# Third stage of a two-layer decoder on one core: the product of memory scores and decay goes from VectorE to GpSimd

## What is computed

```
lfm   = csum[:, :, :, None] - csum[:, :, None, :]        # csum of log sigmoid(forget gate)
log_D = where(lower triangle, lfm, -inf) + ig[:, :, None, :]
D     = exp(log_D - max(log_D, axis=-1))
C     = (q @ k.T / 4 + k_hop) * D                         # the product that is moved
h     = C / (max(|sum(C)|, exp(-max log_D)) + 1e-6) @ v
h     = per-head layer norm of h
x     = layernorm(x + h)
```

## Time and profile before

| | us |
|---|---|
| runs, median of 3 | 4131.79 (4114.9 to 4133.13) |
| the profiled execution | 4115.69 |
| its span, first to last instruction | 4113.5 |
| third stage, within the span | about 894 to 1890 |

### The profile page before, as it was taken

How to read it: one execution, slowest core, us unless ns; L and a number is a source line. 1 busy time by engine, 2 the same in 40 slices (tenths; PEclk the granted TensorE clock), 3 DMA queues, 4 the chain that set the end, 5 groups by cost and what they waited for, 6 DMA issues and landing times.

```text
span 4113.5 us, 92034 instructions
## 1 busy us (share of the span) xinstructions
PE 2848.6 (69%) x27504; PEld 1910.9 (46%) x27505; DVE 2433.5 (59%) x7020; ACT 1603.5 (39%) x3994; POOL 1878.1 (46%) x2306
## 2 busy tenths in 40 slices
PE   3999999758777887774038878888888850166600
PEld 2666666435444555542026646666666630155500
DVE  2777777438887778886001137777777761144455
ACT  2666666324544444442013335555555520011100
POOL 4222222016665556662740036666666616511167
PEclk9999999968988779885569989999999975599855
DMA  2111111441111111110222211111111102211133
GB/s 54 41 40 40 39 38 42 150 131 42 46 47 41 47 40 47 40 40 20 77 72 68 78 36 30 27 29 28 27 27 28 27 11 64 67 54 56 54 83 87
DMA packets 282376, 207.13 MB, mean 50 GB/s; under 512 B 61730, under 2 KB 246455, under 8 KB 281904
## 3 DMA queue, kind: packets, MB, share of 16 engines
q1 hardware_dynamic: 262960, 164.88, 13.6%
q0 software_dynamic: 19200, 39.62, 3.5%
HBM read 114.99 MB, written 90.18 MB: 50 GB/s over the span
## 4 chain that ended last, share of the span: by engine, by line
issue 21%; PE 13%; POOL 11%; DVE 7%; POOLq 0%; DMA 0%; ACT 0%; DVEq 0%; ACTq 0%
PE scores_ps L1043 3%; POOL rows L2049 2%; POOL shared L2147 2%; POOL got L2094 2%; POOL norm_rstd L1993 2%; POOL shared L1997 1%; PE heads_ps L1050 1%; PE desk_ps L1050 1%; PE scores_ps L1159 1%; DVE row_max L1567 1%; PE scores_ps L1161 1%; PE heads_ps L1159 1%; PE desk_ps L1159 1%; DVE shared L1902 1%; POOL k_bd L1997 1%
## 5 line engine op out<-in xcount | busy, mean ns | idle before, releaser
L1993 POOL TENSOR_TENSOR norm_rstd<-norm_veps,minus_half 128x1 f32<-128x1 f32 x384 | 233.5, 608 | 509.8 <-DVE norm_veps L1549 509.8
L2049 POOL DMA_INDIRECT rows<-e_in,slot_put x256 | 249.0, 973 | 164.0 <-issue 107.4
L1274 ACT ACTIVATE turned<-scores_ps 128x512 f32<-128x512 f32 x384 | 227.7, 593 | 174.2 <-PE scores_ps L905 168.3
L1567 DVE TENSOR_REDUCE row_max<-scores_ps 128x8 f32<-128x512 f32 x384 | 262.2, 683 | 28.1 <-issue 13.8
L1270 ACT ACTIVATE probs<-probs 128x512 f32<-128x512 f32 x384 | 240.8, 627 | 91.6 <-DVE probs L1569 91.1
L1569 DVE TENSOR_TENSOR probs<-scores_ps,row_max 128x512 f32<-128x512 f32 x384 | 265.5, 691 | 13.2
L905 PE MATMUL scores_ps<-consts,probs 128*128 128x128 f32 x1536 | 250.8, 288 | 16.6 <-ACT probs L1270 12.7
L1202 ACT ACTIVATE probs<-probs 128x512 f32<-128x512 f32 x256 | 161.3, 630 | 136.6 <-DVE probs L1488 134.2
L1486 DVE TENSOR_REDUCE row_max<-scores_ps 128x8 f32<-128x512 f32 x256 | 174.9, 683 | 61.2 <-PE scores_ps L756 56.4
L905 PEld LDWEIGHTS scores_ps<-consts,probs 128*128 128x128 f32 x1536 | 183.9, 148 | 27.3 <-ACT probs L1270 18.3
L1902 DVE COPY shared<-turned_ps 128x256 f32<-128x256 f32 x72 | 30.5, 424 | 263.9 <-PE turned_ps L1151 263.9
(11 more groups left out here) (337 smaller groups left out, 8303.6 us busy)
## 6 DMA issues: line engine op xcount, KB each, us to landing
hop_dram<-shared SPq DMA_DIRECT2D x64, 256.0 KB, 2.1
hop_in<-hop_dram SPq DMA_DIRECT2D x64, 256.0 KB, 3.0
rows<-zero_rows SPq DMA_DIRECT2D x64, 144.0 KB, 1.9
shared<-rows SPq DMA_DIRECT2D x72, 128.0 KB, 2.1
moe<-shared SPq DMA_DIRECT2D x72, 128.0 KB, 1.9
rows<-zero_rows SPq DMA_DIRECT2D x64, 128.0 KB, 1.8
c_in<-in_ctx SPq DMA_DIRECT2D x128, 64.0 KB, 1.9
c_two<-in_ctx SPq DMA_DIRECT2D x128, 64.0 KB, 2.2
```

The costliest lines, as they stand in the source:

```text
L1274: act.activation(turned[a][:, 512 * g:512 * g + 512], scores_ps[:, a, g, :], ACT.Identity)\
L1567: dve.tensor_reduce(best, sc, AX, ALU.max).then_inc(at.shift.sem, 1)
L1993: pool.tensor_tensor(n_rstd[:, k, u, :], n_veps[:, k, u, :], minus_half[:, 0:1], ALU.pow).then_inc(sig.sem, 1)
L2049: pool.indirect_dma_start(out=rows, out_offset=bass.IndirectOffsetOnAxis(ap=slot_put[:, c, U * n + i:U * n + i + 1], axis=0), in_=put_rows ...
```

## The change

The product of tile i+1 leaves DVE's period, where it stood between the statistics of z and the application of y's norm. It enters GpSimd's period between the 1024-column spread of the keys of tile i-1 and the power for y of tile i-3. DVE gets a wait ahead of `decay_logs`, for the product of the tile two back, which read the same half of `decay`. Values, buffers and all other instructions stay.

```diff
                 if live(i + 1):
+                    after(dve, m_shift.of(i - 1))
                     decay_logs(i + 1, 1 - u)
...
                     stats5(mixed, 11, 0, i, u, z[u])
-                if live(i + 1):
-                    after(dve, decayed.of(i + 1, 1), m_shift.of(i + 1, 4))
-                    dve.tensor_tensor(probs[0][:, 0:512], probs[0][:, 0:512], decay[1 - u], ALU.mult).then_inc(m_shift.sem, 1)
                 if live(i - 3):
                     apply5(f_norm, 2, 1 - u, x_out[1 - u], y[1 - u], f_rstd.of(i - 3), h_turned.of(i - 5),
...
                     spread5(k_ring[2 + 1 - u], rope_k[1 - u], "head16").then_inc(f_spread.sem, 1)
+                if live(i + 1):
+                    after(pool, decayed.of(i + 1, 1), m_shift.of(i + 1, 4))
+                    pool.tensor_tensor(probs[0][:, 0:512], probs[0][:, 0:512], decay[1 - u], ALU.mult).then_inc(m_shift.sem, 1)
                 if live(i - 3):
                     after(pool, f_norm.of(i - 3, 4))
                     rstd5(f_rstd, 2, 1 - u)
```

## The result

| | before | after |
|---|---|---|
| runs, median | 4123.73 us (4 runs, 4114.9 to 4133.13) | 4212.56 us (4 runs, 4205.15 to 4228.31) |
| profiled execution | 4115.69 us | 4208.25 us |
| its span | 4113.5 us | 4206.5 us |
| first to last product of the stage | 973.1 us | 1057.3 us |

The medians are 89 us apart. The ratio of the runs is 1.0237, with a 95% interval from 1.0211 to 1.0263: 98 us (87 to 108) of the 4124. The forecast was 4172 us, 40 us more than before. The direction was right, the size less than half.

A forecast was written before the change was run, and what follows sets the result against it. It took DVE's stream with GpSimd's powers as the bound in short steps, PE at low clock in long ones. 36 us of delay plus 4 for the clock gave 4156 us profiled, 4172 as median; range 4136 to 4218.

The forecast's parts named there:

- Which step bounds what: Third stage: DVE's stream with its waits for GpSimd's powers bounds short steps; PE at low clock bounds longer ones.
- What is removed: 64 products of 0.693 us leave DVE, at most 39 us; no gain if what follows is not ready earlier.
- The chain: On GpSimd product, power for y, r4 and power for z precede r_tmp, which starts 0.89 us later in short steps.
- The Trainium skill's rule for GpSimd: Product on GpSimd: 1.39 us by this rule, some 14 us more in all; the forecast took 1.04 us.
- The lock: Shared SBUF interface: a two-input VectorE instruction and a GpSimd one exclude each other; the new product adds nothing to the sum.
- PE's L984 waits no longer: PE's wait for the product in the third stage: gone, as it ends at 1211.42 us instead of 1211.55.
- The sum without the clock: Delays less waits: 27 short steps 26 us, 23 middle 10, 13 long 0; together 36, bounds 26 and 52.
- For the clock I add 4: TensorE's clock in the third stage: more idle time lowers it, costing 4 us, less than one more long step.
- Rival 1: Clock falls more often in the third stage: 5 to 13 further long steps, 4190 to 4230 us; chance 0.17.
- Rivals 2 and 4: Rival 2: early exponential hides the delay, 4135 us, chance 0.16; rival 4: DVE's relief counts, 4093 to 4116 us, 0.04.
- The range: Median of the changed kernel's runs: 4136 to 4218 us; the main forecast's own range was 4150 to 4192.

The follow-up runs named there:

- behind_r4: The changed kernel with the product on GpSimd moved behind the power for y and r4, ahead of the power for z: 4126.56 us, 1.0025.
- behind_z: The changed kernel with the product on GpSimd moved behind the power for z, ahead of the one for the normed x: 4176.30 us, 1.0149.

## Why the prediction was wrong

- **Which step bounds what.** Right. In short steps DVE's stream with GpSimd's powers is the bound; at held clock nearly every step becomes one.
- **What is removed.** Right: 0.61 us a step off DVE bought nothing in the short steps. DVE stands 1.45 us ahead of x_out in the step shown.
- **The chain.** Right in its mechanism, and the place confirms it: the power for y and r4, moved behind the product, cost 0.9 us a short step. The delay was forecast as 0.89 us and is 1.20 (2.37 less 1.17). 0.23 of the difference is the product, 1.27 us instead of 1.04; the rest is that it starts 0.35 us ahead of the variance's end, where I had 0.44. A short step grew a little less, by 1.12 us (14.17 to 15.29), since z's scaling became 0.15 us shorter. The other signs followed in size: DVE's wait for GpSimd ahead of x_out and r_tmp is 2.4 us per period, where 1.8 was forecast, and the stage 1084 us, where 1032 was.
- **The Trainium skill's rule for GpSimd.** That it is about twice as slow as VectorE for an operation with two inputs ("GPSIMD Engine Reference" of the Trainium skill, section 4.1, Engine selection) gave an estimate of 1.39 us against the row's 1.04. The measured 1.27 is 1.83 times VectorE's 0.693, and lies nearer to that rule. I said that the row disagreed with it; the row was of another form.
- **The lock.** It cost nothing on the path in the changed kernel, as argued: there it is x_out that runs beside r4, 0.46 us instead of 0.34, and r_tmp waits for the power for z anyway. What I had looked at was too narrow, z and operations with two inputs. x_out and r_tmp have one input from SBUF, and they too took longer beside GpSimd: x_out 0.96 us in behind_r4, r_tmp 1.28 in behind_z, where it does lie on the path. The same section of the Trainium skill ("SBUF — State Buffer", "Who interferes with whom") counts such operations, tensor_scalar in a mode that uses both port pairs, among those that can contend, and says that whoever issues first has the shared pair for the whole instruction. The traces agree: the product had started first in both, and x_out and r_tmp ended 0.08 us after it.
- **"PE's L984 waits no longer".** Wrong, though small: the product ends 0.92 us after z's variance (1346.67 less 1345.75) instead of 0.73, and PE waits for it 14.4 us in 41 periods instead of 6.2 in 6.
- **The sum without the clock.** 36 us, bounds 26 and 52. At held clock the difference measured is 53 to 58. With the product at its true price, 0.23 more in some 50 steps, 36 becomes 47. That is the part of the path, and it was mis-sized by the product and, as far as the interval lets one say, by somewhat too much absorbed.
- **The failed step: "For the clock I add 4".** It is 35 to 40. The argument had both halves, that the stage lives between two levels and that more idle time can only bring the clock down, and then counted "less than one more such step", because I thought of the lost clock as further long steps of 19 us. Of those there are no more than before (6 of 19 us and more, before 7). What came was low clock in 22 of the 63 steps that last 16 to 17.3 us, about 7 or 10 us of it in most of them, on the path from the attention's output to the log decay. There even 3.4 us of low clock made a step 1 us longer or more, while behind xn they cost about 0.2: the price of the clock hangs on where it is low, and my count of long steps had no such term. Nor did the waits absorb as assumed: PE's matmuls, which had waited for xn once, now did so 38 times.
- **Rival 1** had the mechanism, and its band of 4190 to 4230 us holds the result; it got 0.17. Its sign by which to know it, a clock below 0.79 in the stage, came true (0.78). Rivals 2 and 4 are excluded by the steps: 3 of 63 stayed at 14.35 us or less, where 27 had been. In the step shown the exponential ends 0.42 us ahead of z's variance (1345.33, 1345.75), not earlier than before.
- **The range** ended at 4218, and 4212.56 lies in it, by luck: it stood on a median before of 4131.79 us, and with the 4123.73 of the comparison it would have ended at 4210. The forecast of 40 us was under half of what came.

## What to carry to other kernels

An operation that is moved onto an engine with room is priced by what it now stands ahead of in that engine's order, and by what it then runs beside: behind two small operations the same product cost about 10 us (1.0025) instead of 98 (1.0237), and one place further, where it ran beside r_tmp and TensorE waited for it, about 61 (1.0149). Where TensorE's clock is already mixed, a delay on the path has a second price, here 35 to 40 us beside 55; measure it by filling TensorE's waits with small products in both versions. That filling by itself made the kernel before 0.8% faster (4078.65 us), the fastest kernel of this study, and twice as much of it made it slower.

## What the runs showed of the hardware

- In the step shown the clock fell to the lower level when no wait of TensorE's matmuls in the 13 us at the higher level had been above 0.89 us (0.74, 0.42, 0.69, 0.24, 0.89 and 0.55). The 0.89, ahead of xn, was not there before the change. It took no single long gap.
- One input from SBUF did not keep an operation of VectorE clear of GpSimd: x_out took 0.96 us instead of 0.34, and r_tmp 1.28 instead of 0.35, beside GpSimd's product, and ended 0.08 us after it.
- GpSimd's multiplication of 128x512 values took 1.27 us with two dense operands, in place, and 1.04 us with the second operand broadcast in its innermost dimension; 2.1 ns a column in the dense form.
- z's scaling on DVE took 0.28 us (median) instead of 0.42, once r4 no longer ran beside it on GpSimd; in behind_r4, where r4 is back in its place, it took 0.43.
